# Where the last view of the first token group is rounded to fp8: at the front's end, or at the head of the attention pass

## The reference, cut to what matters

```python
def _div_clamp_fp8(x, scale):
    y = jnp.clip(x.astype(jnp.float32) / scale, -FP8_MAX, FP8_MAX)
    y = y.astype(jnp.bfloat16).astype(jnp.float32)
    return _fp8_roundtrip(y)
...
ln_out = _ln(hidden_states, ln_w, ln_b)
q  = _fp8_linear_pertensor(ln_out, wq,  wq_scale,  q_in_scale)    # view 0
k  = _fp8_linear_pertensor(ln_out, wk,  wk_scale,  k_in_scale)    # view 1
v  = _fp8_linear_pertensor(ln_out, wv,  wv_scale,  v_in_scale)    # view 2
qx = _fp8_linear_pertensor(ln_out, wqx, wqx_scale, qx_in_scale)   # view 3
core = softmax(q k^T) v          # own keys and values
xout = softmax(qx kx^T) vx       # keys and values of the context
```

## Time and profile before

| | |
|---|---|
| median of 3 runs | 664.03 us (663.5 to 665.32) |
| the profiled execution | 660.22 us, of which the span is 658.5 us |
| mean granted TensorE clock | 0.964 |
| PE busy | 582.2 us, 88% |
| DVE busy | 502.7 us, 76% |
| ACT busy | 376.9 us, 57% |
| POOL busy | 364.3 us, 55% |

### The profile page before, as it was taken

One profiled execution on the slowest core, in us unless ns is written; L12 is line 12 of the kernel. 1 busy time (PEld: TensorE's weight loads), 2 busy tenths in 40 slices (PEclk: granted clock), 3 DMA queues, 4 the chain that ended last, 5 costly groups with the idle time before them and its releaser, 6 DMA issues.

```text
span 658.5 us, 10625 instructions
## 1 busy us (share of the span) xinstructions
PE 582.2 (88%) x3738; PEld 469.8 (71%) x3738; DVE 502.7 (76%) x931; ACT 376.9 (57%) x666; POOL 364.3 (55%) x299
## 2 busy tenths in 40 slices
PE   3788888948959999999989899999999899999995
PEld 2554333625538888888878788888889788888884
DVE  3689998785798898998977889999997946333332
ACT  1654767965676765776675756676565235433220
POOL 2321285003547777768677866666767633855331
PEclk9989998987979999999998999999999999999998
DMA  7971112214233121131093142222120100410001
GB/s 237 302 268 48 59 67 87 76 48 131 81 111 129 33 84 45 34 128 33 1 342 99 56 129 65 81 82 71 28 81 17 33 0 3 123 40 12 1 1 64
DMA packets 44563, 54.86 MB, mean 83 GB/s; under 512 B 8416, under 2 KB 30816, under 8 KB 44512
## 3 DMA queue, kind: packets, MB, share of 16 engines
q1 hardware_dynamic: 44512, 54.20, 25.2%
HBM read 41.60 MB, written 12.58 MB: 82 GB/s over the span
## 4 chain that ended last, share of the span: by engine, by line
PE 49%; DVE 8%; POOL 8%; issue 5%; ACT 3%; DMA 1%; SPq 1%; DVEq 0%; POOLq 0%; ACTq 0%
PE g_proj L2291 9%; PE g_proj L2206 7%; PE g_scores L2247 5%; PE g_turn L2236 4%; POOL g_cat L1637 4%; PE g_op L2273 3%; POOL g_rs L1618 3%; PE g_op L474 2%; PE g_op L476 2%; PE g_op L475 2%; PE g_proj L459 2%; PE g_proj L461 2%; PE g_proj L460 2%; POOL g_krs L1623 1%; PE g_scores L459 1%
## 5 line engine op out<-in xcount | busy, mean ns | idle before, releaser
L1618 POOL TENSOR_TENSOR g_rs<-g_ve,neg_half 128x4 f32<-128x4 f32 x80 | 84.2, 1069 | 48.8 <-DVE g_ve L1728 48.5
L2206 PE MATMUL g_proj<-w_hi,g_xqc 128*128 128x512 f32 x192 | 85.1, 443 | 15.2 <-ACT g_qn L1996 6.8
L1637 POOL TENSOR_TENSOR g_cat<-g_yb,g_kb 128x1024 fp32r<-128x1024 bf16 x32 | 70.8, 2221 | 38.6 <-DVE g_yb L1785 38.6
L2206 PE MATMUL g_proj<-w_lo,g_xqc 128*128 128x512 f32 x192 | 77.3, 402 | 0.0
L1970 ACT ACTIVATE g_sq<-g_proj 128x512 f32<-128x512 f32 x80 | 47.6, 597 | 45.6 <-PE g_proj L2206 44.3
L502 POOL TENSOR_TENSOR m_h_lo<-m_h,m_h_hi 128x512 fp32r<-128x512 f32 x32 | 41.4, 1296 | 57.8 <-ACT m_h_hi L489 57.8
L1728 DVE TENSOR_REDUCE g_ve<-g_sq 128x4 f32<-128x516 f32 x80 | 54.5, 682 | 17.9 <-ACT g_sq L1970 16.8
L2247 PEld LDWEIGHTS g_scores<-g_qkT 128*128 128x128 f32 x512 | 60.8, 194 | 4.8 <-issue 3.2
L2247 PE MATMUL g_scores<-g_qkT 128*128 128x64 f32 x512 | 62.6, 276 | 1.7 <-ACT g_qkT L2004 0.9
L2236 PE MATMUL g_turn<-ident,g_qn 128*128 128x128 f32 x384 | 58.9, 276 | 3.5 <-ACT g_qn L1996 1.9
L2236 PEld LDWEIGHTS g_turn<-ident,g_qn 128*128 128x128 f32 x384 | 46.1, 143 | 17.2 <-ACT g_qn L1996 4.3
(11 more groups left out here) (242 smaller groups left out, 1649.4 us busy)
## 6 DMA issues: line engine op xcount, KB each, us to landing
kvx_rows<-f_kept SPq DMA_DIRECT2D x24, 256.0 KB, 2.4
g_ksq<-kvx_rows SPq DMA_DIRECT2D x8, 512.0 KB, 4.4
g_kraw<-kvx_rows SPq DMA_DIRECT2D x16, 256.0 KB, 3.5
g_v<-kvx_rows SPq DMA_DIRECT2D x8, 512.0 KB, 5.2
m_raw<-in_L_W SPq DMA_DIRECT2D x16, 256.0 KB, 3.1
c_raw<-in_L_wqT SPq DMA_DIRECT2D x4, 512.0 KB, 9.0
f_w_ctx<-in_L_wkvxT SPq DMA_DIRECT2D x4, 512.0 KB, 7.7
x_raw<-in_L_wqxT SPq DMA_DIRECT2D x4, 512.0 KB, 4.4
```

The costliest lines, as they stand in the source:

```text
L1618: G.tensor_tensor(rs[:, at % 2, :], ve[:, at % 2, :], k["half"][:, 0:4], ALU.pow).then_inc(q["rs_done"], 1)
L1637: G.tensor_tensor(cat[:, h].rearrange("p h (b s) -> p b h s", b=2), yb[:, h, :].rearrange("p (b h s) -> p b h s", b=2, s=SEQ), kb[:, h, :] ...
L2206: last = T.matmul(bank(n, i)[:], xqc[:, n % 2, view * KT + c_, :], w[:, c_, :], start=c_ == 0 and part == 0, stop=c_ == KT - 1 and part == 1)
```

## The change

The rounding of view 3 of the first group leaves the front. ScalarE's `over_scale` writes u = 6 and 7 not to the ring but to their place in `xq`, unrounded. At the head of the pass VectorE rounds them there in place with a new function, `early_tokens()`, which stands in `ahead` behind `own.low(6)` and ahead of the wait for `eps_made` and `sums(0,0)`. It has five instructions on 128x1024 and uses `kb[:, 1]` for the powers. Five semaphores are new. Two waits are new: `copy_tile(8)`, the first copy of view 3, waits for the last of the five instructions, and so does `late_tokens(1)` ahead of its mask, the first that writes to `kb[:, 1]` otherwise.

```diff
@@ front, VectorE
             round_two(2)
             ln.apply(dve, 5, lambda j: qn[:, 1, j, :])
             round_two(4)
-            round_two(6)
@@ front, ScalarE, over_scale
-                A.activation(yb[:, u % RING, :], lnT[s][:, w % KT, :], ACT.Copy, scale=inv[:, w:w + 1]).then_inc(q["over_done"], 1)
+                out = yb[:, u % RING, :] if w < 3 * KT else k["xq"][:, 3, w % KT, s * N:(s + 1) * N]
+                A.activation(out, lnT[s][:, w % KT, :], ACT.Copy, scale=inv[:, w:w + 1]).then_inc(q["over_done"], 1)
@@ grouped_attention, semaphores: early_clipped, early_abs, early_power, early_big, early_done added
@@ grouped_attention, GpSimd, copy_tile
                     if n == ST:
                         pool.wait_ge(q["late_done"], 4)
+                    if n == TILES:
+                        pool.wait_ge(q["early_done"], 1)
@@ grouped_attention, VectorE
+                def early_tokens():
+                    y, power_ = k["xq"][:, 3, :, 0:ST * P], kb[:, 1, :].rearrange("p (c n) -> p c n", c=KT)
+                    V.tensor_scalar(y, y, FP8_MAX, -FP8_MAX, ALU.min, ALU.max).then_inc(q["early_clipped"], 1)
+                    dve.wait_ge(q["early_clipped"], 1)
+                    V.tensor_scalar(power_.bitcast(U16), y.bitcast(U16), 0x7F80, None, ALU.bitwise_and).then_inc(q["early_abs"], 1)
+                    dve.wait_ge(q["early_abs"], 1)
+                    V.tensor_scalar(power_, power_, FP8_NORMAL, FP8_LIFT, ALU.max, ALU.mult).then_inc(q["early_power"], 1)
+                    dve.wait_ge(q["early_power"], 1)
+                    V.tensor_tensor(y, y, power_, ALU.add).then_inc(q["early_big"], 1)
+                    dve.wait_ge(q["early_big"], 1)
+                    V.tensor_tensor(y, y, power_, ALU.subtract).then_inc(q["early_done"], 1)
@@ late_tokens
                     if view > 1:
                         dve.wait_ge(q["late_done"], view - 1)
+                    if view == 1:
+                        dve.wait_ge(q["early_done"], 1)
@@ ahead, VectorE
                     own.low(dve, 6, True)
+                    early_tokens()
                     dve.wait_ge(q["eps_made"], 1)
                     sums(n, 0)
```

More of the change, by code:

```diff
@@ L1473, in grouped_attention @@
                  "pn_done", "q1_done", "clipped", "abs_done", "k_done", "big_done", "cat_done", "x_done", "ve_done", "rs_done",
-                 "ctx_done", "ctx_kept", "stored0", "stored1", "stored2", "stored3", "over_done", "late_clipped", "late_abs", "late_power", "late_big", "late_done", "k_loaded0", "k_loaded1", "kn_loaded", "ksq_done", "kve_done", "krs_done", "v_loaded0", "v_loaded1", "hi_stored", "lo_stored", "back1", "back2", "back3")
+                 "ctx_done", "ctx_kept", "stored0", "stored1", "stored2", "stored3", "over_done", "early_clipped", "early_abs", "early_power", "early_big", "early_done", "late_clipped", "late_abs", "late_power", "late_big", "late_done", "k_loaded0", "k_loaded1", "kn_loaded", "ksq_done", "kve_done", "krs_done", "v_loaded0", "v_loaded1", "hi_stored", "lo_stored", "back1", "back2", "back3")
         q = {n: take(f"g_{n}") for n in names}
```

## The result

The changed kernel takes 659.46 us (median of 6 runs, 658.33 to 663.65) against 664.16 before (6 runs, 662.37 to 665.32). The ratio is 0.9948, with a 95% interval of 0.9923 to 0.9973: faster by 1.8 to 5.1 us. The forecast was 661.5, or -2.55.

A forecast was written before the change was run, and what follows sets the result against it. TensorE sets the pace overall, but VectorE's `round_two(6)` holds the seam between front and attention pass. Removing it gives -2.55, the added block costs 0; from a median of 664.03 that makes 661.5 us, range 658.9 to 665.0.

The forecast's parts named there:

- Step 1: At the front's end, removing `round_two(6)` lets VectorE, last at the barrier, end earlier: -2.55 us.
- The 0.21 of room to ScalarE: At the seam, ScalarE's end at 146.04 was put 0.21 us ahead of VectorE's new end, 146.25.
- Step 3: At the head of the pass, the five added VectorE instructions of `early_tokens()` take 2.71 us.
- Step 4: Behind the added instructions: `sums(0,0)` 0.95 us late, 1.76 of 2.71 lying in idle time, TensorE's turn 0.20 late.
- Step 5: After the head, whether the 0.20 reaches the end: between 0 and 0.07 us, taken as 0.
- The sum: For the whole kernel, seam and added block together: -2.55 + 0 = -2.55 us.
- the load of output weights as the limit: At the head, the load landing at 162.14 releases `own_out.high(2)` at 162.16; ScalarE's queue is ready at 162.03.
- rival B: At the head, the added block's 0.95 us goes through in full: 662.4 us; chance 0.08.
- Rival A: TensorE's clock falls elsewhere after the shift: 658.2 us for the better, 666.5 for the worse; chance 0.14 each.
- Rival C: At the head, the in-place chain takes 9.2 us rather than 2.71 through strided operands: 668.0 us; chance 0.03.
- D: At the seam, another participant holds the restart at 150.18, so nothing is gained: 664.0 us; chance 0.05.
- the prediction's sentence on a later place: A few microseconds later in the pass, the block would have paid about 2 us to GpSimd's port lock.

The follow-up runs named there:

- seam only: The changed kernel with the five new instructions left out, view 3 of the first group staying unrounded: 660.95 us against 663.2 for the kernel before, ratio 0.9949.
- high later: The changed kernel with ScalarE's `own_out.high(2)` moved behind `square(0,3)`: 661.37 us against 664.2 for the kernel before, ratio 0.9954.
- block three times: The changed kernel with its five new instructions run three times one after another: 668.11 us against 663.2 for the kernel before, ratio 1.0069.
- head lows: The changed kernel with ScalarE's `own_out.high(2)` behind `square(0,3)` and GpSimd's `low(2)` and `low(3)` behind `rstd(0,5)`: 659.93 us, ratio 0.9945 to the kernel before.
- last rounding twice: The kernel before with `round_two(6)` run a second time at the front's end: 664.08 us against 664.2, ratio 1.0015.
- block later: The changed kernel with the five new instructions moved to between `sums(0,3)` and `late_tokens(0)`: 667.2 us against 664.2 for the kernel before, ratio 1.0048.

## Why the prediction was right

**Right, by its own steps.** Step 1: VectorE was last at the seam; 2.55 predicted, 2.56 in the trace. Three traces of the changed kernel and the seam-only one all have 5.30 from the normalisation to the restart. The 0.21 of room to ScalarE was real and thin: where TensorE transposed at the slow level (1.94 for the eight, against 1.62 in the earlier trace rows), ScalarE ended last and the distance was 5.43 ("high later"; 5.41 in "block three times" and "head lows"), so 0.13 can be missing. Step 3: 2.71 predicted, 2.71 measured, and the strided view in place costs nothing (0.41, 0.43 and 0.69 for the clip, the masks and the two last). Step 4: 0.95 late at `sums(0,0)` predicted, 0.96 measured; turn 0.20 late predicted, 0.22 measured. Step 5, that none of it reaches the landmarks behind the head: 12.00 against 11.98, and the third copy at the same distance. The sum, -2.55, lies in the interval of all three comparisons of the changed kernel; that nothing else comes with it is shown to about 1 us by the times (ratios 0.9948, 0.9962 and 0.9961, or -3.5, -2.5 and -2.6). That the first comparison came to 659.46, 2.0 below the forecast and near the edge of its range, is scatter and no merit of the sum.

**Wrong in what held the head.** The prediction took the load of output weights as the limit and named, as a sign against it, that `own_out.high(2)` would be released by ScalarE's own queue. It was, in all three traces of the changed kernel. The prediction let ScalarE's queue be free when the last eviction ended, 0.13 before the load; but the next instruction starts 0.48 behind an eviction's start, not 0.60, so the two limits were 0.25 apart. The eviction came 0.27 later (11.52 behind the restart against 11.25), and that put ScalarE's queue in front, by 0.02. This was a tie and not a cover, and that 12.00 meets 11.98 is partly luck: in the changed kernel's own execution the load lands at about 162.0, 0.3 before the instruction starts. Its issue comes 7.0 to 7.9 behind the restart, as one small issue of SP ahead of it takes 0.43 or up to 2.14 us. Without the block the head can go 0.6 faster when load and full clock come early ("seam only"); in the kernel before, "last rounding twice" and "block later" the load held it at 11.98, 11.87 and 12.02. So the block isn't free: rival B is true at up to 0.6 in some executions, and at about zero in others; the times can't show so little.

**Rival A** (the clock) is there in size: stretches of 3.4 us that cost 1.6 to 1.7 each, two of them in each trace of the changed kernel, which by themselves take back more than the seam gives. In the timed runs no such sign is seen: slow time beside the 2.55 is 1.7 more in one comparison and 2.0 less in the other. Why all three traces of the changed kernel have the same two falls stays open. **Rival C** (slow in-place chain) and **D** (another participant holds the seam) fell with the first trace. As for **C**'s price, the run with the block three times shows that beyond the cover the price is 1.3 per microsecond and not 1: the idle time it adds also brings TensorE's clock down.

What the prediction's sentence on a later place had right was the lock at 2.85, and wrong that it would be added: GpSimd's one subtraction blocks only one lift. It also left out the larger part, the block's own 2.7 without cover and the slow clock behind it; about 6 instead of about 2.

## What to carry to other kernels

In front of a barrier, work that only one engine still does is on the path in full, and behind it there can be a stretch where the same engine waits for the others' first results, as here. Moving work across was worth the whole difference in arrival here; there was 0.21 of room to the next latest engine. Price the cover at the new place by following the delayed instruction to where two waits meet, and when they are within a few tenths call it a tie, since the hidden one takes over. When the scatter of one execution is larger than the change, compare distances from a landmark that both traces have, and count the slow clock time separately before believing a span.

## What was not expected of the hardware

- An execution's time follows TensorE's slow time, at about 0.35 us per us, and slow time varies from 37 to 64 us between runs of one and the same kernel ("last rounding twice"), at otherwise the same instructions. A stretch of 3.4 appears or not behind the same short wait: at 527, after 2.5 us idle, there was none before and one after.
- One small DMA issue on SP's queue behind the restart, the second small parameter's, took 1.35 to 2.14 us in nine of the thirteen traces; in the other four it took 0.43, and the next one 1.27 to 1.54. The other small ones all take 0.43 to 0.47. It helps to decide which of two waits holds the head.
- The engines restarted 1.38 to 1.41 us behind the end of the engine that came last at the seam, in each trace, whoever that was.
